# Query and key blocks of a second attention layer: one operation per engine, rows by DMA, score maxima moved among the products

## What is computed

```python
qkv = x @ w_qkv.T + b_qkv            # x is 2 x 1024 x 512 after layernorm, q, k, v of 256 features each
q, k, v = split(qkv, 3)              # 8 heads of 32
scores = einsum('bhfc,bhtc->bhft', k, q)      # f: key, t: query; masked to f <= t
attn = softmax(scores, axis=-2)
vals = einsum('bhft,bhfc->bhtc', attn, v)
out = vals @ w_o.T + b_o
```

## Time and profile before

| What | us |
|---|---|
| Three timed runs | 1346.51, 1352.97, 1356.73 (median 1352.97) |
| The profiled execution, its own time | 1344.81 |
| Its span, first to last instruction | 1343.1 |
| Mean granted TensorE clock in it | 0.928 of full |
| Busy in it: PE, DVE, ACT, POOL | 1205.7 (90% of the span), 953.5, 671.2, 375.2 |

### The profile page before, as it was taken

One profiled execution on the slowest core, in us unless ns is written; L12 is line 12 of the kernel. 1 busy time (PEld: TensorE's weight loads), 2 busy tenths in 40 slices (PEclk: granted clock), 3 DMA queues, 4 the chain that ended last, 5 costly groups with the idle time before them and its releaser, 6 DMA issues.

```text
span 1343.1 us, 21792 instructions
## 1 busy us (share of the span) xinstructions
PE 1205.7 (90%) x6800; PEld 753.2 (56%) x6800; DVE 953.5 (71%) x2990; ACT 671.2 (50%) x1023; POOL 375.2 (28%) x505
## 2 busy tenths in 40 slices
PE   4998999999899877998879999999988988879988
PEld 1875444443388865444868744444435887744368
DVE  5889889898166676653659798999962667576365
ACT  2621666666655452544436036666665554435542
POOL 0431411122254400114614323122213542002162
PEclk9996899999999997999979858999999999869999
DMA  8374411220010020100140742112200100120001
GB/s 317 120 196 87 125 29 26 57 65 3 1 49 1 1 47 19 55 2 0 63 175 23 189 130 70 26 26 57 66 2 0 50 1 17 32 72 2 1 8 56
DMA packets 37285, 76.20 MB, mean 57 GB/s; under 512 B 5084, under 2 KB 6620, under 8 KB 37036
## 3 DMA queue, kind: packets, MB, share of 16 engines
q1 hardware_dynamic: 37176, 74.82, 19.2%
HBM read 48.98 MB, written 27.08 MB: 57 GB/s over the span
## 4 chain that ended last, share of the span: by engine, by line
PE 64%; DVE 19%; issue 5%; POOL 5%; ACT 5%; DMA 1%; DVEq 0%; SPq 0%; ACTq 0%; POOLq 0%
PE bank L999 16%; PE bank L871 12%; PE bank L779 5%; PE bank L780 5%; PE bank L781 5%; DVE maxes L1208 5%; PE bank L983 4%; PE bank L977 3%; DVE unused L1204 3%; PE bank L765 3%; DVE ops L1152 3%; PE bank L881 2%; POOL x L1484 2%; POOL w_odd L1466 2%; ACT ops L1356 2%
## 5 line engine op out<-in xcount | busy, mean ns | idle before, releaser
L1431 ACT ACTIVATE probs<-bank 128x1024 f32<-128x1024 f32 (+3 forms) x416 | 367.9, 911 | 320.4 <-PE bank L983 220.3
L871 PE MATMUL bank<-ops 48*128 48x512 f32 (+3 forms) x960 | 321.8, 436 | 34.5 <-DVE maxes L1204 17.2
L1204 DVE CUSTOM_DVE_ANT_0 unused<-bank,causal 128x128 bf16<-128x128 f32 (+3 forms) x640 | 279.5, 486 | 47.7 <-PE bank L871 44.1
L1542 POOL TENSOR_SCALAR_AFFINE_SELECT probs<-probs 128x256 f32<-128x256 f32 (+1 forms) x256 | 118.8, 464 | 640.3 <-ACT probs L1431 640.0
L871 PEld LDWEIGHTS bank<-ops 48*128 48x128 f32 (+1 forms) x960 | 163.0, 206 | 218.9 <-DVE maxes L1204 96.0
L999 PE MATMUL bank<-probs,v_mem 128*17 128x512 f32 (+6 forms) x1920 | 252.2, 517 | 6.1 <-ACT heads_raw L1418 5.6
L1208 DVE TENSOR_REDUCE maxes<-bank 128x1 f32<-128x512 f32 x320 | 207.4, 684 | 40.7 <-PE bank L871 39.2
L983 PE MATMUL bank<-ops 50*128 50x512 f32 (+2 forms) x640 | 175.9, 448 | 5.0 <-ACT probs L1431 4.8
L779 PE MATMUL bank<-ops,xT 128*128 128x512 f32 (+1 forms) x288 | 116.2, 403 | 19.6 <-DVE x L1068 11.6
L983 PEld LDWEIGHTS bank<-ops 50*128 50x128 f32 x640 | 86.6, 197 | 57.9 <-ACT probs L1431 29.5
L1473 POOL TENSOR_TENSOR rstd<-var_eps,minus_half 128x1 f32<-128x1 f32 x96 | 52.7, 549 | 215.1 <-DVE var_eps L1046 214.5
(11 more groups left out here) (117 smaller groups left out, 1965.5 us busy)
## 6 DMA issues: line engine op xcount, KB each, us to landing
query_rows_dram<-ops SPq DMA_DIRECT2D x48, 256.0 KB, 3.8
ops<-query_rows_dram SPq DMA_DIRECT2D x64, 192.0 KB, 4.4
w_odd<-staging_wqkv SPq DMA_DIRECT2D x4, 1536.0 KB, 7.3
x<-x_dram SPq DMA_DIRECT2D x16, 256.0 KB, 6.1
ops<-ops SPq DMA_DIRECT2D x16, 256.0 KB, 3.0
out_dram<-x SPq DMA_DIRECT2D x16, 256.0 KB, 2.0
staging_wqkv<-wqkv_dram SPq DMA_DIRECT2D x2, 1536.0 KB, 15.8
key_rows_dram<-ops SPq DMA_DIRECT2D x24, 128.0 KB
```

Source lines behind the costliest of these rows:

```text
L871: last = mm(dst[:, h * w:(h + 1) * w], queries(a, u)[rows, t // 4, hi, t % 4 * P:(t % 4 + 1) * P], keys(a, u, hi)[rows, HALF * kp:HALF * k ...
L1204: V.tensor_tensor_reduce(unused[:, masked % 3, 0:w], part, causal[:, HALF - w:], 1.0, NEG, ALU.add, ALU.max, dst).then_inc(s["max_done"].s ...
L1431: A.activation(probs[:, e % 6, :, 0:cols], scores[:, 2 * (e % 2):2 * (e % 2) + 2, 0:cols], ACT.Exp, scale=a.scale).then_inc(s["exp"].sem, 1)
L1542: G.affine_select(out=p, in_=p, compare_op=ALU.is_ge, fill=0.0, base=0, pattern=pattern, channel_multiplier=-1).then_inc(s["masked"].sem, 1)
```

## The change

In the second layer only:

1. ACT reads a block once: one operation on 128 rows into a staging buffer (in `heads_raw`, two in turn), with the bias. DVE waits for it and makes the low part of all 128 rows in one operation into `features`; with that the bank is free. The high rows of heads 0 and 1 are copied to their place by DVE, those of heads 2 and 3 by ACT, four copies of 32 rows from SBUF to SBUF.
2. The low rows are laid in place by four DMAs of 32 rows each, and the second high rows by one DMA as before: five DMAs on SP for a block, in `rows_of_block`. Ring items wait for all five. The first shift rows are issued behind six blocks, the second behind all eight.
3. Twenty-one ring items stand among the products, from heads tick 4 on, two of them among value products; one is left for just before the first scores. In a tick of value products DVE reads a ring item behind each product.
4. In attention two value steps are issued on end, in every even step, instead of one in each.
5. `bias_head1` and its load are gone.

```diff
-            self.ring_in = {5: (0, 0, 1, 1), 6: (1, 1, 1, 1), 8: (0, 0, 1, 1), 9: (1, 1, 2, 2)}
+            self.ring_in = {4: (0, 0, 1, 1), 5: (1, 1, 1, 1), 7: (0, 0, 1, 1), 8: (1, 2, 2, 2), 9: (1, 2, 2, 1)}
...
+            def rows_of_block(b, j, g):
+                s, rows, m = qs[QKV1], part_rows[j, g], block_no1(j, g)
+                _, low = staged1(j, g)
+                sp.wait_ge(s["read"].sem, s["read"].at(b, A1.product_no("qk", j, g) + 1))
+                for h in range(4):
+                    _, lo = head_rows1(j, h, g)
+                    sp.dma_start(lo.bitcast(F32), low[32 * h:32 * (h + 1), :]).then_inc(rows.sem, 16)
...
+                sp.wait_ge(s["hi"].sem, s["hi"].at(b, m + 1))
+                sp.wait_ge(high_half.sem, high_half.at(b, m + 1))
+                sp.dma_start(mem[to:to + 32], mem[0:32]).then_inc(rows.sem, 16)
...
-                copy_high(b)
+                for j, g in ((0, 0), (1, 0), (3, 0), (0, 1), (1, 1), (3, 1)):
+                    rows_of_block(b, j, g)
                 load_shifts(b, QKV1, 0, 0)
+                for j, g in ((2, 1), (2, 0)):
+                    rows_of_block(b, j, g)
                 load_shifts(b, QKV1, 0, 1)
...
-                            pe.wait_ge(s["read"].sem, s["read"].at(b, a.product_no("qk", j, g) + 1))
-                            pe.wait_ge(copied[j, g].sem, copied[j, g].at(b, 16))
+                            pe.wait_ge(part_rows[j, g].sem, part_rows[j, g].at(b, 16 * 5))
...
+                    elif g % 2 == 0 and g > a.lag and g - a.lag < a.units * ns:
+                        value(g - a.lag - 1)
                         value(g - a.lag)
...
-                    dve.wait_ge(s["hi"].sem, s["hi"].at(b, sum(p[0] == "qk" for p in a.products[:m + 1])))
-                    for h in range(4):
-                        hi, lo = head_rows1(j, h, g)
-                        last = V.scalar_tensor_tensor(lo, src[32 * h:32 * (h + 1), :], bias_head1[:, 4 * j + h:4 * j + h + 1],
-                                                      hi.bitcast(F32), ALU.add, ALU.subtract)
-                    last.then_inc(s["read"].sem, 1)
+                    n, (high, low) = block_no1(j, g), staged1(j, g)
+                    dve.wait_ge(high_staged.sem, high_staged.at(b, n + 1))
+                    V.scalar_tensor_tensor(low.bitcast(F32R), src, bias_qk1[:, j:j + 1], high, ALU.add, ALU.subtract
+                                           ).then_inc(s["read"].sem, 1)
+                    for h in range(2):
+                        hi, _ = head_rows1(j, h, g)
+                        last = V.tensor_copy(hi, high[32 * h:32 * (h + 1), :])
+                    last.then_inc(high_half.sem, 1)
...
-                for h in range(4):
+                n, (high, _) = block_no1(j, g), staged1(j, g)
+                if n >= 2:
+                    act.wait_ge(high_half.sem, high_half.at(b, n - 1))
+                A.activation(high.bitcast(F32R), qkv_banks[m % 3], ACT.Identity, bias=bias_qk1[:, j:j + 1]
+                             ).then_inc(high_staged.sem, 1)
+                act.wait_ge(high_staged.sem, high_staged.at(b, n + 1))
+                for h in range(2, 4):
                     hi, _ = head_rows1(j, h, g)
-                    last = A.activation(hi, qkv_banks[m % 3][32 * h:32 * (h + 1), :], ACT.Identity,
-                                        bias=bias_qk1[32 * h:32 * (h + 1), j:j + 1])
+                    last = A.copy(hi, high[32 * h:32 * (h + 1), :])
                 last.then_inc(s["hi"].sem, 1)
```

More of the change, by code:

```diff
@@ L328, in build @@
         bias_qk1 = sb("bias_qk1", [P, 4])
-        bias_head1 = sb("bias_head1", [32, 16])
         bias_v = {QKV0: sb("bias_v0", [P, 128]), QKV1: sb("bias_v1", [P, 256])}
@@ L446, in build @@
         rope_stored = [signal(f"rope_stored{n}", 96) for n in range(6)]
-        copied = {(j, g): signal(f"high_copied{j}_{g}", 16) for j in range(4) for g in range(2)}
+        part_rows = {(j, g): signal(f"part_rows{j}_{g}", 16 * 5) for j in range(4) for g in range(2)}
+        high_staged = signal("high_staged", 8)
+        high_half = signal("high_half_copied", 8)
         chunks_of = [2 if st == WO1 else KC for st in range(8)]
@@ L521, in head_rows1, with block_no1, staged1 @@
             return (keys(A1, u, i)[32 * n:32 * (n + 1), HALF * g:HALF * (g + 1)] for n in (0, 2))
+        def block_no1(j, g):
+            return [p for p in A1.products if p[0] == "qk"].index(("qk", j, g))
+        def staged1(j, g):
+            n = block_no1(j, g)
+            return heads_raw[:, n % 2, :], features[:, HALF * n:HALF * (n + 1)]
         def rope_sums(eng, ops_of, b, n):
@@ L577, in load_biases @@
                 sp.dma_start(wlora[:, :], W["lora_b"]).then_inc(s_w, 16)
-                for dst, src in ((bias_qk0, W["bias_qk0"]), (bias_qk1, W["bias_qk1"]), (bias_head1, W["bias_head1"]),
+                for dst, src in ((bias_qk0, W["bias_qk0"]), (bias_qk1, W["bias_qk1"]),
                                  (bias_v[QKV0], W["bias_v0"].partition_broadcast(P)),
@@ L824, in heads_product @@
                             last = mm(dst[:, 0:n], x_lo[:, k, :], hi[:, k, a.qk_feats:], start=False, stop=(k == KC - 1))
+                        between()
                 last.then_inc(s["product"].sem, 1)
@@ L1015, in attention @@
                     ring_items(len(a.ring_at[g][1]))
-                    if a.lag <= g < a.units * ns + a.lag:
+                    if a.row_tiles == 2:
+                        if a.lag <= g < a.units * ns + a.lag:
+                            value(g - a.lag)
+                    elif g % 2 == 0 and g > a.lag and g - a.lag < a.units * ns:
+                        value(g - a.lag - 1)
                         value(g - a.lag)
@@ L1115, in heads_read @@
                     if b == 0:
-                        dve.wait_ge(s_qkv_bias, 16 * 5)
+                        dve.wait_ge(s_qkv_bias, 16 * 4)
                     if a.rope:
@@ L1179, in chain @@
                     if tick.heads:
-                        h = i - first_heads
-                        for _ in range(sum(ATT[att].ring_in.get(h, ()))):
+                        in_chunk = ATT[att].ring_in.get(i - first_heads, (0, 0, 0, 0))
+                        single = len(tick.heads) == 1
+                        for _ in range(sum(in_chunk) if single else 0):
                             ring_read(b, att, ring_no)
                             ring_no += 1
-                        for p in tick.heads:
+                        for k, p in enumerate(tick.heads):
                             heads_read(b, att, *p)
+                            for _ in range(0 if single else in_chunk[k]):
+                                ring_read(b, att, ring_no)
+                                ring_no += 1
             def ring_read(b, st, i):
@@ L1226, in ring_read @@
                         dve.wait_ge(s["lo"].sem, s["lo"].at(b, 6))
+                    if c == 0 and not a.rope:
+                        for g in range(2):
+                            for j in (2, 3):
+                                dve.wait_ge(part_rows[j, g].sem, part_rows[j, g].at(b, 16 * 5))
                     V.reciprocal(inv_sum[:, 0:4 * nh].unsqueeze(2), blocks[:, :, d:d + 1]).then_inc(s["inv"].sem, 1)
@@ L1582 @@
         "wqkv1": a["L1_attn_w_qkv"].T[:, A1.feature_order()],
-        "bias_qk1": b_qkv1[:A1.qk_feats].reshape(-1, P).T, "bias_head1": b_qkv1[:A1.qk_feats].reshape(-1, 32).T, "bias_v1": b_qkv1[A1.qk_feats:],
+        "bias_qk1": b_qkv1[:A1.qk_feats].reshape(-1, P).T, "bias_v1": b_qkv1[A1.qk_feats:],
         "wo1": a["L1_attn_w_o"].T, "bo1": a["L1_attn_b_o"],
```

26 lines of the change are left out of this document (8 added, 18 removed).

## The result

The kernel before took 1353.33 us (median of 6 runs, 1345.41 to 1364.68), the changed kernel 1302.14 (median of 6, 1295.45 to 1314.14). The ratio is 0.963, 95% interval 0.957 to 0.969. The medians differ by 51.2 us; the forecast of 1302 was 51 off the median that was known then, and its sum said 49.9. The profiled execution of the changed kernel took 1308.18, span 1306.5.

The account below looks back on a forecast made before the run. PE sets the time, idling in the product stage behind ACT's and DVE's block operations. Gains of 36.5 and 13.4 sum to 49.9 us: 1295 from the profiled 1344.8, 1303 off the median; forecast 1302, range 1286 to 1322.

Parts of the forecast that it names:

- Part 1: Block reading: ACT 0.68 plus copies of 0.61, DVE 0.75 plus copies of 0.42; bank free after 1.5 us instead of 5.7.
- Part 2: Rows by DMA: each issue takes SP 0.59 us and lands after 3.0; five make 2.9 us of SP a block.
- Part 3: New order from second layer's first product to scores of step 4: gains 19.0 and 17.5 us, together 36.5.
- The clock term of 0.7: Behind the product stage: two waits close together may keep PE at 1.2 GHz longer, costing 0.7 us in the first sequence.
- The waits left: PE waits remaining at the start of attention: 2.5 us ahead of first scores, about 3 ahead of step 4's scores.
- Part 4: Paired value steps in attention: 22 fewer runs at 0.28 us and no heads' copy wait; 6.7 us a sequence, 13.4 in all.
- The 1.5 for the ring's bursts: Attention: ring items between value pairs outrun DVE's reductions, charged 1.5 us a sequence within bounds of none and 14.
- (a): Attention: switching doesn't go away, or the ring's bursts eat the gain; 12.4 us come back, 1315; chance 0.14.
- (b): Product stage: the five row DMAs land after 7.6 us instead of 3.0; 8 us a sequence lost, 1318; chance 0.14.
- (d): Product stage: a block's five DMAs land one behind another, 15 us a block; 24 us slower a sequence, 1400; chance 0.03.
- (e): Product stage: no gain, waits move from DVE to the shift rows and block paths stay as long; 1345; chance 0.05.
- (c): Behind the product stage: PE's clock stays up, winning the slow 9.2 us too; 5 us a sequence, 1292; chance 0.09.

Follow-up runs that it names:

- e4: Changed kernel with DVE's one low-part operation per block split into four on 32 rows each; 0.989 of the kernel before, first product to first scores 61.3 and 60.9 us.
- e7: Changed kernel with ACT's one high-part operation per block split into four on 32 rows each; 0.984 of the kernel before, first product to first scores 58.2 and 58.3 us.
- e11: Changed kernel with old ring places and one value step in each attention step; 0.972 of the kernel before, first product to first scores 45.5 us.
- e1: Changed kernel with one value step in every attention step again, all else as changed; 0.967 of the kernel before.
- e2: Kernel before the change with only the value steps paired; 0.995 of the kernel before.
- e9: Changed kernel with the second layer's ring items scheduled further ahead (ahead=1.14 for 1.07); 0.963 of the kernel before.

## Why the prediction was right

The forecast was 49.9 us for the parts together, and the changed stretches give 48.8 and 49.7. The mechanism is the one named: e4 and e7 show that the length of the chain ACT then DVE set the stage, e11 that shortening it is enough. That the sum is right to 2% is luck: two errors had opposite signs. By e1, reading, rows and ring places are worth 307.3 - 263.3 = 44.0 us where the forecast had 36.5, and the pairs 4.8 where it had 13.4. First scores came at P + 45.2, a little ahead of the 46 to 48 given as the sign of being right.

- **Part 1, the prices**: right, each within 0.01 us: 0.687, 0.746, 0.411 and 0.618. The Trainium skill, "VectorE: DVE Perf Modes", section "What auto-detection actually checks", would have a copy between two SBUF tiles at two elements a cycle, float32 included; by the row of 0.411, beside the 0.416 of line 1290, that holds here with the output of the rounded type too.
- **Part 2, landing**: taken as 3.0, is 2.0 for the low rows, 3.0 for the high ones. The 2.0 shortened nothing on the path, since the high rows are issued last: the row at 504.93 shows item 6 released by their DMA (`ops<-ops`), issued at 501.75. It waits 0.7, not 1.6, for the reasons in the next point.
- **Part 3, the walk**: up to the value products it is exact (their end at P + 13.2). From there it runs late: item 6 at +31.1 (walk 32.1), PE's last product at +43.0 (44.3), first scores at +45.2 (46.85), scores of step 4 at +50.9 and +51.7 (53.1). Two terms were mis-sized. The narrower reductions, "put at 0.5 to 0.8 an item", are cheaper at the narrow end: a masked operation of 128 columns takes 0.29 and its reading out 0.08, so that DVE frees (1,1) at P + 25.4 (walk 26.2) and has the last maxima 0.6 us behind PE's last product, not 1.1. And the walk let the 3.0 of landing begin at the end of the last issue, while the profile counts them from its start: 0.4 less, of which issues that come a little more than 0.59 apart take 0.2 back. Together with the 0.8 of (1,1) this is the 1.0 at item 6. Item 18 waits for DVE's maxima as walked, 0.6 for 0.5. From P to the scores of step 4 the gain is 23.0 and 20.6 us where the walk had 20.7 and 19.2. The clock term of 0.7 has the right size (behind S the time at 1.2 GHz was 8.9 and 8.4 us, is 10.2 in both, and half of 1.3 and 1.8 is 0.7 and 0.9) for a wrong reason: I had laid it to two waits close together, and with the first of them alone, in e1, that time is 6.8.
- **The waits left**: 2.5 ahead of the first scores, is 2.25. "About 3" ahead of step 4, is 0.94 in the first sequence and 2.12 in the second. In the first PE comes to these scores as walked (P + 49.95 for 50.1), but the copy of the shifts ends 1.6 us earlier and the rows take 2.8 from there, not 3.4. In the second they stand behind the last block's issues on SP for 1.2 us, which the prediction names as a possibility and doesn't price.
- **Part 4, the pairs**: the step that failed. From the scores of step 4 to V the gain is 2.9 and 2.3 us a sequence, not the 6.7 less 1.7 that I had. By e1 the pairs are worth 2.0 to 3.0 a sequence. Three terms are mis-sized. "A run of value steps therefore costs 0.28 beyond its columns" is 0.23, 5.1 us a sequence for 6.2. The 2.0 for the heads' copy, won as forecast, is taken back by waits for the shift rows of 2.0 and 3.2, which I had seen only for the first unit: in every unit the transposed shifts stand in the ring behind a value pair, and no value step is left between scores 3 and 4 to cover the DMA. e2 and e9 show both sides of it: it comes with the pairs, and it goes when the ring runs further ahead. And the longer time at the lower clock, 1.7 us against single steps, I had charged to the waits of part 3 at 0.7; it goes with the pairs behind the scores. The 1.5 for the ring's bursts doesn't show: PE waits for no maximum from 518 to 604, and for 0.2 us in the second sequence; only its weight loads, which overlap the products, wait for them.
- **Rivals.** (a) is half true: the switching does go away, but little more than a third of part 4's 13.4 us is kept (4.8 to 5.7). (b) and (d) are refuted by the landing of 2.0 and 3.0 us, (e) by e11. (c) is refuted: the clock is 0.53 behind the first scores though the stage before ran at 1.00, so the high clock of the stage was not kept over the wait of 2.25 us and the scores behind it.

My recorded expectations for e4 and e7 were too low by half and more. I had thought that the changed stage had slack, as PE is idle in it for 3.5 us and waits for three banks in turn. What I missed is that the chain holds PE again as soon as it is longer, in six or seven places of the stage and not behind the last two blocks alone, and that the idle time then costs clock as well (4.7 and 5.2 us of the 16.1 and 13.0).

## What to carry to other kernels

Where several operations on slices of the partitions stand between a product and its freed bank, put them into one on all partitions, even if that takes copies and small DMAs afterwards: here the chain until the bank was free set the time, while the copies ran beside the next product. Count what such DMAs add to the issuing queue: rows that are wanted soon stand behind them. Before grouping work to save switches, look for what the single steps covered: a wait that had a value step in front of it shows only when that step moves. And where executions differ by more than the effect, compare the changed stretches between two marks in the traces, and look at the granted clock of the executions before explaining a difference of 8 us.

## What the hardware showed that I had not expected

- The price of a pass by itself was expected; that it holds on both engines to within 1% is new: DVE 746 ns on 32 and on 128 rows (e4), ACT 680 and 687 (e7).
- A copy of 64 KB from SBUF to SBUF lands 2.0 us after its issue, one of 256 KB after 3.0, and four small ones issued on end, 0.59 us each, still land in 2.0 by the median (1.9 to 3.0 over all 64).
- The granted clock over 215 us of unchanged code was 0.97 in one execution and 0.90 in another, which carries most of a shift of 10 us, a fifth of what the whole change is worth.
